# Moving work off the end of a counting stage, and another choice of the basis buffer that stands apart

## What is computed

```
m   = relu(concat(h[src], edge_attr) @ W1.T + b1) @ W2.T + b2
agg = segment_sum(m, dst)                       # then a GRU cell and a batch norm
w   = einsum('rb,bio->rio', att, basis)         # 30 basis matrices 512x512 -> 2 relations, in two layers
msg = sigmoid(x[col] @ gate_w[r]) * x[col] @ w[r]   # r by the edge's type
out = segment_sum(msg, row) + x @ root + bias   # relu between the two layers
```

## Time and profile before

| | |
|---|---|
| median of three runs | 502.38 us |
| the profiled execution's own time | 498.94 us |
| its span | 497.1 us |
| TensorE busy | 470.2 us (95%) |
| VectorE busy | 296.1 us (60%) |
| ScalarE busy | 204.2 us (41%) |
| mean granted clock | 0.981 |

### The profile page before, as it was taken

One profiled execution on the slowest core, in us unless ns is written; L12 is line 12 of the kernel. 1 busy time (PEld: TensorE's weight loads), 2 busy tenths in 40 slices (PEclk: granted clock), 3 DMA queues, 4 the chain that ended last, 5 costly groups with the idle time before them and its releaser, 6 DMA issues.

```text
span 497.1 us, 6857 instructions
## 1 busy us (share of the span) xinstructions
PE 470.2 (95%) x2310; PEld 318.2 (64%) x2310; DVE 296.1 (60%) x578; ACT 204.2 (41%) x365; POOL 102.2 (21%) x116
## 2 busy tenths in 40 slices
PE   7988969999999999999999999996899999999995
PEld 2433436666666665975676686663666688788884
DVE  5885797989899898484021589864113115442323
ACT  1885874555545554372044214663232014242000
POOL 0000175668776630000000410000000060000000
PEclk9998988999999999999999999998899999999999
DMA  8997676888898854989798799669877450200011
GB/s 255 431 372 260 232 208 183 290 259 265 296 300 277 279 188 179 399 334 366 289 382 338 287 317 383 260 232 415 317 316 282 193 170 3 84 1 1 22 44 42
DMA packets 29640, 121.21 MB, mean 244 GB/s; under 512 B 4331, under 2 KB 7355, under 8 KB 25247
## 3 DMA queue, kind: packets, MB, share of 16 engines
q1 hardware_dynamic: 17950, 92.33, 49.6%
q0 software_dynamic: 7856, 24.91, 15.9%
q10 hardware_dynamic: 3792, 3.43, 2.3%
HBM read 113.85 MB, written 6.82 MB: 243 GB/s over the span
## 4 chain that ended last, share of the span: by engine, by line
PE 77%; DMA 11%; DVE 6%; issue 2%; DVEq 1%; ACT 0%; SPq 0%
PE ps L1444 16%; PE ps L1499 12%; PE ps L1286 11%; DMA basis<-in_basis 11%; PE ps L1322 10%; PE ps L1537 9%; PE ps L1370 4%; PE ps L1374 4%; PE ps L1371 3%; PE ps L1482 3%; PE ps L1311 2%; PE ps L1252 1%; DVE x L998 1%; PE ps L1264 1%; DVE X L925 1%
## 5 line engine op out<-in xcount | busy, mean ns | idle before, releaser
L1286 PE MATMUL ps<-basis,sel 128*32 128x512 f32 x496 | 60.4, 620 | 7.1 <-DMA basis<-in_basis 7.1
L1322 PE MATMUL ps<-xT_lo,xT_hi 128*128 128x512 f32 x237 | 62.5, 411 | 3.4 <-DVE xT_hi L984 2.0
L619 POOL DMA_DIRECT2D X<-w_layer x32 | 16.8, 656 | 208.7 <-DMA w_layer<-ev 208.7
L610 POOL DMA_INDIRECT X<-u_rows,esrc x40 | 43.4, 1085 | 77.9 <-DMA u_rows<-X 57.5
L1322 PEld LDWEIGHTS ps<-xT_lo,xT_hi 128*128 128x128 f32 x237 | 43.9, 194 | 19.0 <-issue 7.0
L1537 PE MATMUL ps<-Xr,CT_r 128*128 128x512 f32 x200 | 47.0, 389 | 0.0
L610 POOL DMA_INDIRECT x_sb<-u_rows,esrc x39 | 40.8, 1047 | 16.3 <-DVE x L998 8.4
L1157 DVE SCALAR_TENSOR_TENSOR Xr<-ps,gate,Xr 128x512 fp32r<-128x512 f32 x20 | 14.9, 750 | 48.0 <-ACT Xr L792 48.0
L1537 PEld LDWEIGHTS ps<-Xr,CT_r 128*128 128x128 f32 x200 | 37.5, 188 | 7.8
L693 ACT ACTIVATE rhi<-x 128x512 fp32r<-128x512 f32 x60 | 35.3, 631 | 14.4 <-DVE x L998 14.2
L1286 PEld LDWEIGHTS ps<-basis,sel 128*32 128x32 f32 x496 | 14.9, 111 | 39.4 <-issue 28.3
(11 more groups left out here) (231 smaller groups left out, 818.4 us busy)
## 6 DMA issues: line engine op xcount, KB each, us to landing
basis<-in_basis SPq DMA_DIRECT2D x29, 2048.0 KB, 10.0
X<-in_eaT SPq DMA_DIRECT2D x20, 256.0 KB, 4.4
basis<-in_basis SPq DMA_DIRECT2D x8, 512.0 KB, 6.9
X<-w_layer POOLq DMA_DIRECT2D x32, 128.0 KB, 3.0
w_layer<-ev SPq DMA_DIRECT2D x13, 256.0 KB, 11.2
X<-in_WhhT SPq DMA_DIRECT2D x3, 1024.0 KB, 15.1
basis_apart<-in_basis SPq DMA_DIRECT2D x1, 2048.0 KB, 19.7
X<-in_WihT SPq DMA_DIRECT2D x2, 1024.0 KB, 10.8
```

The lines of the kernel that those rows point to most:

```text
L610: nc.gpsimd.indirect_dma_start(gat[e % GATHERS], None, t["u"][:, :], bass.IndirectOffsetOnAxis(ap=esrc[:, e:e + 1], axis=0)).then_inc(gat_ ...
L1286: mm = pe.matmul(bank[32 * g:32 * g + 32], sel[:, layer, s], held[:, g, s2], start=(s == 0), stop=(s == 3), tile_position=(0, 32 * g))
L1322: mm = pe.matmul(ps[:, EA_BANKS[s]], part[:, u % 2, s * P:(s + 1) * P], w, start=(i == 0), stop=(i == 2))
```

## The change

In the basis part, the third buffer now holds load 2 (the first half of tile 1), and SP asks in turn for load 3, load 4 and, later, load 5. Load 4 now goes into slot 0, free since window 4.

At the end of the counting, unit 1's attributes are split in the windows 15 (ACT) and 16 (DVE). The last window's copy is shared: ACT takes partitions 0 to 63, DVE 64 to 127. `fold` is made in unit 6. PE clears four of the five banks ahead of `attributes(0, 3)`, and the last one (bank 1, of the last window) where all five were cleared.

```
-SPLIT_AT = (11, 13)
+SPLIT_AT = (11, 13, 15)
-APART = 4
+APART = 2
@@ sync
-            for c in range(SLOTS, 2 * SLOTS):
+            for c in (APART + 1, APART + SLOTS):
                 load_basis(sp, c)
             store_sources(NT - 3)
             load_attributes(0)
-            for c in range(APART + 1, EARLY * SLOTS):
-                load_basis(sp, c)
+            load_basis(sp, EARLY * SLOTS - 1)
@@ scalar
-                if w == SPLIT_AT[1]:
-                    upper_attributes(0)
+                if w in SPLIT_AT[1:]:
+                    upper_attributes(SPLIT_AT[1:].index(w))
...
-            upper_attributes(1)
+            w = WINS - 1
+            act.wait_ge(ct_acc, WINS)
+            for q in range(FOLD // 2):
+                nc.scalar.copy(CT[WIN * (w % FOLD):WIN * (w % FOLD + 1), w // FOLD, q * SPAN:(q + 1) * SPAN],
+                               ps[WIN * q:WIN * (q + 1), w % 3, 0:SPAN])
+            nc.scalar.copy(win_cnt[0:P // 2, w:w + 1], ps[0:P // 2, w % 3, SPAN:SPAN + 1]).then_inc(last_drained, 1)
@@ vector
-                if w == SPLIT_AT[1] + 1:
-                    dve.wait_ge(ea_hi_ready, 1)
-                    dve.tensor_tensor(ea_lo[:, 0], eaT[:, 0], ea_hi[:, 0].bitcast(F32), ALU.subtract
-                                      ).then_inc(ea_ready, 1)
+                if w - 1 in SPLIT_AT[1:]:
+                    lower_attributes(SPLIT_AT[1:].index(w - 1))
...
+                if u == 6:
+                    dve.tensor_reduce(fold, ident[:].rearrange("p (q d) -> p d q", q=FOLD), AX.X, ALU.add
+                                      ).then_inc(fold_ready, 1)
...
-            for q in range(FOLD):
+            for q in range(FOLD // 2, FOLD):
                 dve.tensor_copy(CT[at, w // FOLD, q * SPAN:(q + 1) * SPAN], ps[WIN * q:WIN * (q + 1), w % 3, 0:SPAN])
-            dve.tensor_copy(win_cnt[:, w:w + 1], ps[:, w % 3, SPAN:SPAN + 1]).then_inc(last_drained, 1)
-            dve.tensor_reduce(fold, ident[:].rearrange("p (q d) -> p d q", q=FOLD), AX.X, ALU.add
-                              ).then_inc(fold_ready, 1)
-            lower_attributes(1)
+            dve.tensor_copy(win_cnt[P // 2:P, w:w + 1], ps[P // 2:P, w % 3, SPAN:SPAN + 1]).then_inc(last_drained, 1)
@@ tensor
-            def clear_sums():
-                pe.wait_ge(early_drained, EARLY)
-                for n in (3, 4, (WINS - 3) % 3, (WINS - 2) % 3, (WINS - 1) % 3):
...
+            def clear_bank(n):
+                pe.matmul(ps[:, n], zer[:, 0:P], zer, start=True, stop=True)
...
                 if u == 0:
-                    clear_sums()
+                    pe.wait_ge(last_drained, 2)
+                    clear_bank((WINS - 1) % 3)
...
+            pe.wait_ge(early_drained, EARLY)
+            clear_bank(3)
+            clear_bank(4)
+            pe.wait_ge(ct_drained, WINS - 2)
+            clear_bank((WINS - 3) % 3)
+            pe.wait_ge(ct_drained, WINS - 1)
+            clear_bank((WINS - 2) % 3)
             pe.wait_ge(wins_ready, 1)
             attributes(0, UNIT - 1)
```

More of the change, by code:

```diff
@@ L914, in _, with lower_attributes @@
             ahead = window_span(dve, 0)
+            def lower_attributes(u):
+                dve.wait_ge(ea_hi_ready, u + 1)
+                dve.tensor_tensor(ea_lo[:, u % 2], eaT[:, u % 2], ea_hi[:, u % 2].bitcast(F32), ALU.subtract
+                                  ).then_inc(ea_ready, 1)
             def hot_codes(slot, w, first, tiles):
@@ L979, in _ @@
                                                    in1=bias_raw, op0=ALU.mult, op1=ALU.add).then_inc(bias_ready, 1)
[L981 to L985, removed]
             def add_rows(u, tiles):
```

## The result

Over 20 runs of each, the changed kernel takes 501.68 us (496.42 to 507.29) and the kernel before 503.54 (498.78 to 510.15). The ratio is 0.995, 95% interval 0.9926 to 0.9975: faster, by some 2.5 us, where 6.9 were forecast. The direction was right and the size was not; the range, 493.3 to 499.6, does not hold the time.

The account below looks back on a forecast made before the run. PE was taken to set the time nearly everywhere. Basis loads 3.7, end of windows 3.5, less 0.3 for fold, give 6.9 us: 502.38 to 495.5, likeliest range 494 to 497.5, with the first two rivals 493.3 to 499.6.

Parts of the forecast that it names:

- The wait near 42 us goes, the clock stays up.: Basis loads, tile 1's second half: load 3 lands at 41.25, before PE wants it at 42.03; worth 3.7 us.
- Load 5 about 52, against 55.3; the queue should be empty by then as it was before.: Later basis loads: load 5 lands about 52, wanted at 55.3, and SP's queue is empty for the source stores behind.
- Gathers up to 56.5 cost nothing and each microsecond after costs one.: POOL's first gather, expected at 55.5: a start up to 56.5 is free, each microsecond later loses one.
- B: End of the windows and hand-over to the units: DVE's addition moves from 82.22 to 78.7, a gain of 3.5 us.
- Whether ACT and DVE can read the bank at once: Last window's shared copy: both read one PSUM bank together in different partitions; if one behind the other, 2.5 us, not 3.5.
- Fold costs 0.3.: Unit 6, where DVE and PE are nearly even: the moved 0.36 us instruction loses 0.3 us, bounds 0 and 0.4.
- Behind that the chain is PE with waits that start from its own progress, so the gains should go through to the end.: From the units onward: no later wait absorbs the gains, so the full 6.9 us reaches the end.
- the first two rivals: Load 3 is still late, 499.2, chance 0.12; the hand-over to the units gives little, 498.0, chance 0.12.
- Its last rival: The change's two parts cancel or are hidden by a later fixed wait, about 502; chance 0.04.

Follow-up runs that it names:

- thin_again: The changed kernel with the unit stage's basis quarter loads cut to 16 of 128 partitions, timed once more: ratio 0.988 to the kernel before.
- stores_act: The changed kernel with the stores of sources 2 to 4 issued by ACT instead of SP: a gain of 1.0% on the faster device.
- thin_quarters: The changed kernel with the unit stage's basis quarter loads cut to 16 of 128 partitions, first timing: ratio 0.9889 to the kernel before.
- spread: The changed kernel with SP's burst of attributes, W2T row and basis quarter taken apart: ratio 0.9895 on the faster device, 0.9961 on a slower one.
- spread3: The changed kernel with load 3 in the third buffer and SP's bursts taken apart: 0.9879 (490.16 us) on the faster device, 0.9984 on a slower one.
- b_only: The kernel before with only the end-of-windows edits and fold in unit 6, basis loads in the old order: ratio 0.9974.
- before_third: The kernel before, unchanged, profiled again on a slower device, where before takes 503.4 to 505.4 us.

## Why the prediction was wrong, by its steps

1. *The wait near 42 us goes, the clock stays up.* Right. Load 3 was there; PE reached the source rows at 44.39 instead of 48.24, 3.9 us earlier; the forecast was 3.7.
2. *Load 5 about 52, against 55.3; the queue should be empty by then as it was before.* Wrong, and the first step that failed. Load 5 landed near 56.2, 12.4 us after its issue. The transfer engines were idle from 32 to 34 and then carried loads 3, 4 and 5 (6.3 MB) and some 2 MB more without a pause. I added 5 us behind load 4 and left out what I had named myself, the stores and attributes between, and the rate at which all of it moves. The cost is the wait for load 5: 1.0 us here, up to 1.5 in the other profiles with the same loads, none in thin_again. The first gather came at 58.45 instead of 55.5.
3. *Gathers up to 56.5 cost nothing and each microsecond after costs one.* The second half is wrong: the later gathers cost nothing either. DVE's first additions start 9.76 us behind the second half of tile 2, within 0.01, in the change, stores_act, thin_quarters, thin_again, spread and spread3, with first gathers from 55.51 to 59.35. On the faster device the leads differ by load 5's wait: 5.8 us with 1.47 us of it (spread) and 7.2 with none (spread3).
4. *B = 3.5 us.* Right in its rows. Moved window-16 split, four early clears, two copies, full clock behind them: all as described. DVE's addition ran at 75.87; the forecast was 78.7 less 3.7, 75.0, and the difference is the 1.0 us of step 2. Of the 6.3 us at unit 1, 2.8 stand already at tile 2 (56.24 for 59.01), and 3.5 are B. Whether ACT and DVE can read the bank at once is hardly tested: ACT's half ran from 67.02 to 68.03 and DVE's from 67.91.
5. *Fold costs 0.3.* Right: from unit 6's closing matmul to unit 7's it is 5.68 us in the profile after and 5.44 before.
6. *Behind that the chain is PE with waits that start from its own progress, so the gains should go through to the end.* This is the step that took most of the gain. It holds on the faster device, where the lead of unit 1 stands at unit 18 within 0.8 us in every profile and the edited kernels with both parts gain 1.0 to 1.2%, 5.6 to 6.5 us in the medians. It fails on the slower ones. There DVE's addition of the twelfth tile waits 3.3 to 4.7 us for counts whose matmuls end 3 to 5.6 us before DVE can go on, PE then waits for DVE, and with the lower clock behind it this takes 5.4 to 6.8 us in unit 2 alone. So the waits do hang on PE, as the prediction had it; what it took for nothing is the time from PE's matmul to the engine that waits for its count, because it read the profile of one execution in which that time is under 0.1 us in this whole stretch. That execution, at 498.94, is faster than all but one of its kernel's 20. The gathers' lead over DVE did shrink, from 12.7 to 7.3 us in the twelfth tile, but no row shows that this cost anything.

The chances of the forecast and the first two rivals, 0.69 and 0.24, make 0.93, where the prediction has 0.92. Its last rival says that the chain shows no later wait from anything but PE's progress; the wait for a basis load near 340 us was not looked at, and in b_only it took the whole lead.

Why PE's counts come late on the slower devices, and why in units 2, 10 to 12 and 15 of the changed kernel, stays open. So does the account of the 2.5 us: on the slower devices both kernels lose, the change 11.6 to 13.3 us between the units 1 and 18 and before_third 1.9 us there and more in the windows. The medians of the first 20 runs differ by 1.9 us, the ratio says 2.5, and three profiles of the change on slower devices cannot be averaged against one of before.

## What to carry to other kernels

When a profile can't name what ended a wait, list every counter that the waiting instruction needs, and look at when each was raised; then look for a wait of the same kind where the suspect isn't needed at all, as at L920 here. A stage that asks for several large loads is to be summed in bytes over the rate seen when the engines are full, from the moment of the first issue, small transfers included; here moving a store to another queue changed nothing, and moving a load's issue into an idle stretch did. One profile of a kernel whose runs spread over 2% is one draw, and the median of the next measurement belongs to the device as well.

## What the runs showed that I had not expected

- The same program takes 496.7 us on one device and 503.4 to 505.4 on two others, medians of 17 to 35 executions each. Two edited kernels that gain 1.05 and 1.2% on the first (spread, spread3) gain 0.4 and 0.2% on another, where neither is clear of no change.
- On the slower two, counts that PE raises can reach the trace, and DVE, up to 5.6 us after the matmul that raises them, several together; on the faster one always within 0.1 us, from 60 us to the end of the units.
- A store of 256 KB took 5.1 us on SP's queue and about as long on ACT's (53.09 to near 58), both behind a full set of engines, against 2.0 us before, at a DMA share of 0.35.
- The first gather can start at 55.5 or at 59.35 without moving DVE's first additions against PE.
